# Attention layer on one core: swapping partitions by transfers, a later routing transpose, and one exponential for each quad of score banks

## The reference, cut to what matters

```
x  = L0_attn_x
xn = layernorm(layernorm(x)) * ln1_g + ln1_b
q  = rope(l2norm(xn @ Wq));  k = rope(l2norm(xn @ Wk));  v = xn @ Wv
clock = softplus(xn @ clock_w + clock_b)          # one per head
gcp = exp(clip(cumsum(-softplus(xn @ gate_w + gate_b)), -60, 50))
p_exp = exp(p - max(p)) * clock,  p = xn @ p_w + p_b
q = q * gcp / (cumsum(p_exp) + 1e-8)
k = k / (gcp + 1e-8) * p_exp
out = softmax(causal(q @ k.T / sqrt(8))) @ v @ out_w + out_b
x1 = out + residual;  y = x1 + mlp(layernorm(x1));  x = x + layernorm(y)
# the next layer routes each token to one of 8 experts: argmax(layernorm(x) @ centroids.T)
```

## Time and profile before

| what | value |
|---|---|
| median of 3 runs | 2163.32 us (2157.25 to 2165.94) |
| span of the profiled execution | 2164.4 us (no separate time is given for it beside its span) |
| attention's part of the span | from 0 to about 760 us |
| TensorE, VectorE, ScalarE, GpSimd busy, whole span | 85%, 79%, 68%, 54% |
| mean granted TensorE clock | 0.931 of full speed |

### The profile page before, as it was taken

One profiled execution on the slowest core, in us unless ns is written; L12 is line 12 of the kernel. 1 busy time (PEld: TensorE's weight loads), 2 busy tenths in 40 slices (PEclk: granted clock), 3 DMA queues, 4 the chain that ended last, 5 costly groups with the idle time before them and its releaser, 6 DMA issues. The chain is left out here.

```text
span 2164.4 us, 37241 instructions
## 1 busy us (share of the span) xinstructions
PE 1849.2 (85%) x12576; PEld 954.5 (44%) x12600; DVE 1703.8 (79%) x3547; ACT 1474.7 (68%) x2917; POOL 1165.1 (54%) x720
## 2 busy tenths in 40 slices
PE   6999999999998459957889889898898988659996
PEld 2566666656665259952222222222222222124453
DVE  7778868877863437854899999999999998976776
ACT  5888888888885138845656666666666666437775
POOL 2122232242221027871789999999999998840001
PEclk9999999999999669977899999999999998879998
DMA  4100010011001012221100111001111100023333
GB/s 169 36 26 26 28 49 26 26 36 41 21 25 33 20 50 77 88 72 42 30 25 27 34 35 34 27 30 30 31 35 35 35 31 30 21 67 90 97 84 78
DMA packets 103708, 97.35 MB, mean 45 GB/s; under 512 B 9137, under 2 KB 86113, under 8 KB 103137
## 3 DMA queue, kind: packets, MB, share of 16 engines
q1 hardware_dynamic: 95584, 75.34, 12.4%
q0 software_dynamic: 6784, 18.10, 2.5%
q10 hardware_dynamic: 1152, 1.54, 0.2%
HBM read 45.87 MB, written 28.10 MB: 34 GB/s over the span
## 5 line engine op out<-in xcount | busy, mean ns | idle before, releaser
L1935 POOL TENSOR_TENSOR hc<-h,c_rep 128x1024 f32<-128x1024 f32 x256 | 627.8, 2463 | 137.9 <-DVE h L1899 136.7
L1899 DVE TENSOR_TENSOR_SCAN h<-decay,bank 128x1024 f32<-128x1024 f32 x241 | 551.0, 2286 | 22.5 <-issue 0.9
L1757 ACT ACTIVATE decay<-bank,neg_a_r 128x510 f32<-128x510 f32 x512 | 322.6, 683 | 257.5 <-PE bank L1634 257.1
L1618 PE MATMUL bank<-u_in,sel_rows 32*128 32x512 f32 x964 | 287.9, 675 | 95.7 <-DVE h L1899 95.6
L1634 PE MATMUL bank<-delta,sel_rows 32*128 32x512 f32 x1024 | 338.8, 677 | 0.9 <-ACT decay L1757 0.9
L1886 DVE TENSOR_TENSOR bank<-bank,b_rep 128x1024 f32<-128x1024 f32 x241 | 291.2, 1208 | 34.8 <-PE bank L1618 33.0
L992 POOL DMA_INDIRECT rows_in_dram<-row,idx x64 | 63.3, 989 | 318.3 <-DVE row L965 303.7
L574 ACT ACTIVATE es<-bank 128x384 f32<-128x384 f32 x512 | 208.9, 499 | 22.1 <-PE bank L373 21.8
L1618 PEld LDWEIGHTS bank<-u_in,sel_rows 32*128 32x128 f32 x964 | 76.0, 191 | 276.7 <-DVE h L1899 199.7
L1649 PE MATMUL bank<-hc,y_sel 128*32 128x512 f32 x1024 | 149.6, 660 | 0.8 <-POOL hc L1935 0.8
L1656 PE MATMUL bank<-xpad,w_conv 128*128 128x512 f32 x256 | 133.0, 634 | 3.2 <-ACT xc L1819 1.6
(11 more groups left out here) (341 smaller groups left out, 4170.0 us busy)
## 6 DMA issues: line engine op xcount, KB each, us to landing
r_tw<-r_o_t SPq DMA_DIRECT2D x96, 128.0 KB, 2.3
xvs<-xv SPq DMA_DIRECT2D x16, 512.0 KB, 2.9
u_wide<-u_rep_dram SPq DMA_DIRECT2D x30, 256.0 KB, 3.5
xs<-rows_in_dram SPq DMA_DIRECT2D x72, 68.0 KB, 1.8
front<-in_x_dram SPq DMA_DIRECT2D x16, 256.0 KB, 2.9
w<-in_w_dram SPq DMA_DIRECT2D x2, 2048.0 KB
xlb_dram<-front SPq DMA_DIRECT2D x16, 256.0 KB, 2.3
xlb_m<-xlb_dram SPq DMA_DIRECT2D x16, 256.0 KB
```

Of the source, the lines that this page charges most:

```text
L1618: last = pe.matmul(BD[n % 2][:, i * STEP:(i + 1) * STEP], sel[at:at + 32, r, :], u_in[p if n < NS else q][at:at + 32, hf, :], start=True, ...
L1757: act.activation(decay[n % 4][:, i, :, 1:], seq(DL[i])[:, :, 1:], ACT.Exp, scale=c["neg_a_r"][:, hf, g:g + 1]).then_inc(s["n_da"], 1)
L1899: dve.tensor_tensor_scan(flat(h[n % RING]), decay[n % 4].rearrange("p i b t -> p (i b t)"), flat(drive_0) if by_pool else BD[n % 2], 0.0, ...
L1935: pool.tensor_tensor(hc[n % RING][:, :, :], h[n % RING][:, :, :], c_rep[p if n < NS else q][:, :].unsqueeze(1).to_broadcast([P, 2, STEP]), ...
```

## The change

The swapped projections go. `FA` is now multiplied by cos and by sin at once (`f_ra`, `f_rb`), SyncE exchanges the partitions of `rot_b` pairwise into a new buffer `rot_s` with two transfers (every second partition each way), and `f_rq` and `f_rk` subtract `rot_s`. In TensorE's order the q norm (L481) moves between `weigh(6)` and `weigh(7)`, the projection of k in front of `back(3)`, the routing transpose of xl2 behind `quad(2)`, the affinities behind the k norm, the ranks behind `quad(4)`. VectorE's and ScalarE's orders follow, and the routing's small instructions now stand together. The four exponentials of a quad are one over the four banks, and the quad raises `s_score` once, after its fourth bank. GpSimd's L985 waits for `m_xl2` too. `w_a` is loaded in three pieces without the two swapped blocks, and two small buffers of the end lie in `log`.

The diff, without the declarations, the changed counts of `p_small` (64 to 96) and `s_score` (32 to 8 a pair), and the `es` indexing in `weigh`:

```diff
+        def swap(sp, sem):
+            for to in range(2):
+                sp.dma_start(rot_s[to:P:2, :], rot_b[1 - to:P:2, :]).then_inc(sem, 16)
...
             if front:
+                sp.wait_ge(s["f_rb"], one_on)
+                swap(sp, s["f_qsw"])
+                sp.wait_ge(s["f_kb"], one_on)
+                sp.wait_ge(s["f_rq"], one_on)
+                swap(sp, s["f_ksw"])
                 sp.wait_ge(s["f_xlb"], one_on)
... pe_step
                 quad(7, k - 2, p)
-            if front:
-                pe.wait_ge(s["f_pe"], k + 1)
-                project(FB, c["w_qs"], s["f_qs"])
             if late:
                 weigh(6, k - 2, p)
+            if front:
+                pe.wait_ge(s["f_sq"], k + 1)
+                pe.wait_ge(s["f_rb"], k + 1)
+                pe.matmul(FA[:, :], c["ones_blk"], square[:, :], start=True, stop=True).then_inc(s["f_ssq"], 1)
+            if late:
                 weigh(7, k - 2, p)
             if scores:
                 quad(0, k - 1, q)
+            if front:
+                pe.wait_ge(s["f_pe"], k + 1)
+                project(FB, c["w_k"], s["f_k"])
             if late:
                 back(3, k - 2)
-            if front:
-                pe.wait_ge(s["f_sq"], k + 1)
-                pe.wait_ge(s["f_ra"], k + 1)
-                pe.matmul(FA[:, :], c["ones_blk"], square[:, :], start=True, stop=True).then_inc(s["f_ssq"], 1)
-                pe.wait_ge(s["f_rb"], k + 1)
-                project(FB, c["w_k"], s["f_k"])
...
                 quad(1, k - 1, q)
-            if front:
-                pe.wait_ge(s["f_mq"], k + 1)
-                project(FA, c["w_ks"], s["f_ks"])
             if scores:
                 weigh(0, k - 1, q)
+            if scores:
+                weigh(1, k - 1, q)
+                quad(2, k - 1, q)
             if tail:
                 pe.wait_ge(s["m_xl2"], k - 2)
                 transposes(M, xl2, s["m_x2t"])
-            if scores:
-                weigh(1, k - 1, q)
-                quad(2, k - 1, q)
... act_step
-                for st in range(HS):
-                    act.wait_ge(s["s_score"], u * 32 + HS * n + st + 1)
-                    if st == 0:
-                        since(act, s["s_av"], u * 8 + n - 1)
-                    last = act.activation(es[(n % 2) * HS + st][:, :], RING[st][:, 0:3 * P], ACT.Exp, scale=DH ** -0.5)
-                last.then_inc(s["s_exp"], 1)
+                act.wait_ge(s["s_score"], u * 8 + n + 1)
+                since(act, s["s_av"], u * 8 + n - 1)
+                act.activation(es[n % 2][:, :, :], ring[:, :, 0:3 * P], ACT.Exp, scale=DH ** -0.5).then_inc(s["s_exp"], 1)
... dve_step
                 dve.tensor_tensor(seq(rot), seq(FA), cos, ALU.mult).then_inc(s["f_ra"], 1)
+                since(dve, s["f_ksw"], 32 * k)
+                dve.tensor_tensor(seq(rot_b), seq(FA), sin, ALU.mult).then_inc(s["f_rb"], 1)
             if tail:
                 dve.wait_ge(s["m_st2"], k - 2)
                 bn_aggr(mv_m, stats_m, s["m_mv2"])
...
                 dve.scalar_tensor_tensor(pre[:, 0, :], pre[:, 0, :], 0.0, log[:, 0, :], ALU.max, ALU.add).then_inc(s["f_sp"], 1)
+                dve.wait_ge(s["f_ra"], k + 1)
+                dve.wait_ge(s["f_qsw"], 32 * k + 32)
+                dve.tensor_tensor(rot[:, :], rot[:, :], rot_s[:, :], ALU.subtract).then_inc(s["f_rq"], 1)
... pool_step
                 pool.wait_ge(s["f_back"], k + 1)
+                if tail:
+                    pool.wait_ge(s["m_xl2"], k - 2)
                 pool.tensor_tensor(mag[:, 1, :], mag[:, 1, :], one_up[:, :], ALU.subtract).then_inc(s["f_lost"], 1)
```

More of the change, by code:

```diff
@@ L232, in attention @@
         v_a = [sb(f"v_a{n}", [P, TS, H, 32]) for n in range(2)]
[L234 removed]
+        es = [sb(f"es{n}", [P, HS, 3 * P]) for n in range(2)]
         avs = sb("avs", [P, 512])
@@ L275, in attention @@
         end = sb("end", [1, E])
-        of = sb("of", [1, ETILES])
-        before = sb("before", [1, ETILES])
+        of, before = (log[0:1, 0, n * ETILES:(n + 1) * ETILES] for n in range(2))
         hi = sb("p_hi", [E * FC, P], bf16)
@@ L500, in pe_step @@
                 transposes(M, xl2, s["m_x2t"])
-            if scores:
-                weigh(1, k - 1, q)
-                quad(2, k - 1, q)
-            if tail:
-                pe.wait_ge(s["m_x2t_sb"], k - 2)
-                for j in range(TS):
-                    last = pe.matmul(M[:, j * E:(j + 1) * E], o_t[:, j * P:(j + 1) * P], c["cent"][:, :], start=True, stop=True)
-                last.then_inc(s["m_aff"], 1)
             if scores:
@@ L516, in pe_step @@
             if front:
-                pe.wait_ge(s["f_ka"], k + 1)
+                pe.wait_ge(s["f_kb"], k + 1)
                 pe.wait_ge(s["f_sk"], k + 1)
                 pe.matmul(FB[:, :], c["ones_blk"], square[:, :], start=True, stop=True).then_inc(s["f_ssk"], 1)
+            if tail:
+                pe.wait_ge(s["m_x2t_sb"], k - 2)
+                for j in range(TS):
+                    last = pe.matmul(M[:, j * E:(j + 1) * E], o_t[:, j * P:(j + 1) * P], c["cent"][:, :], start=True, stop=True)
+                last.then_inc(s["m_aff"], 1)
             if scores:
@@ L528, in pe_step @@
                 transposes(M, o_tok[p], s["m_ot"])
+            if scores:
+                weigh(2, k - 1, q)
+                quad(4, k - 1, q)
             if tail:
@@ L541, in pe_step @@
                 last.then_inc(s["r_rank"], 1)
-            if scores:
-                weigh(2, k - 1, q)
-                quad(4, k - 1, q)
             if mid:
@@ L815, in dve_step @@
                 bn_aggr(mv_m, stats_m, s["m_mv2"])
-            if front:
-                dve.wait_ge(s["f_qs"], k + 1)
-                since(dve, s["f_rk"], k)
-                dve.tensor_tensor(seq(rot_b), seq(FB), sin, ALU.mult).then_inc(s["f_rb"], 1)
             if tail:
@@ L906, in dve_step @@
                 dve.tensor_tensor(factor[:, :], factor[:, :], pcs[:, :], ALU.subtract).then_inc(s["f_zq2"], 1)
+            if front:
+                dve.wait_ge(s["f_ssk"], k + 1)
+                dve.wait_ge(s["f_zq"], k + 1)
+                dve.tensor_scalar(lnorm[:, :], FB[:, :], 1e-24, None, ALU.max).then_inc(s["f_mk"], 1)
+                dve.wait_ge(s["f_ka"], k + 1)
+                dve.wait_ge(s["f_ksw"], 32 * k + 32)
+                dve.tensor_tensor(rot_k[:, :], rot_k[:, :], rot_s[:, :], ALU.subtract).then_inc(s["f_rk"], 1)
+                dve.wait_ge(s["f_fq"], k + 1)
+                dve.wait_ge(s["f_rq"], k + 1)
+                since(dve, s["s_score"], 8 * k - 8)
+                dve.tensor_tensor(q_t[p][:, :], rot[:, :], factor[:, :], ALU.mult).then_inc(s["f_qt"], 1)
             if tail:
```

89 lines of the change are left out of this document (39 added, 50 removed).

## The result

The changed kernel takes 2193.91 us (median of 4 runs, 2190.81 to 2198.8) against 2162.13 us for the kernel before, measured beside it (4 runs, 2157.25 to 2165.94): a ratio of 1.0153, 95% interval 1.0133 to 1.0172, or +32 us. The forecast was +14. The sign was right and the time lay inside the range, but the predicted time missed by 17 us, more than the forecast change itself. It also lay above the 2190 that the forecast's own case reached; the range went higher only for the sake of rival D, which is not what happened in the steady steps. That it held is partly luck.

The account below looks back on a forecast made before the run. VectorE's unbroken queue was taken as the bound: -2.15 + 1.1 + 1.4 + 0.45 + 0.2 = +1.0 us a step, +13 over 13 steps, with -1 and +2 at the ends +14, 2177 us. Range 2140 to 2202 us.

Parts of the forecast that it names:

- the forecast's own case: VectorE's queue gets longer: 2177 us, own range 2168 to 2190, chance 0.47.
- rival D: Much slower: TensorE's pauses in a step let its clock fall, 2201 us, chance 0.08.
- Steps 0 to 2: First steps, without routing: no GpSimd collision lost before or after, projections save a little, -1 us together.
- the +2 for steps 16 to 18: Last steps: TensorE waits for the single exponential and the routing stands later, +2 us together.
- Items 1 and 2: VectorE's queue: xl2 freed from GpSimd's pair, -2.15 us a step; the late pair delays the second softplus sum, +1.1.
- Item 3: TensorE's q norm before `weigh(7)` and k projection before `back(3)`: `heads_rec(3)` waits for `back(3)`, +1.4 us a step.
- Item 4: VectorE's seven small routing instructions in a row take 1.25 us instead of 0.8 spread out: +0.45 us a step.
- Item 5: ScalarE's fused exponential: starts after the fourth mask matmul, quad 5's result later, +0.2 us at the step's end.
- Items 6 and 7: Removed k projection on TensorE gains nothing; the swap's transfers land in time: 0 us each on VectorE's queue.
- B: Faster: TensorE's new order costs VectorE nothing, step down 1.6 us, 2142 us in all; chance 0.23.
- C: No change that can be told: GpSimd does not hold up the running sum, 2163 us; chance 0.22.

Follow-up runs that it names:

- b3: Kernel before with the partition exchange by transfers in place of the two swapped projections, `w_a` loaded in three pieces, orders as before: ratio 1.0093.
- b4: b3 with GpSimd's pair waiting for xl2 too: ratio 0.9965 to the kernel before.
- d1: b3 with two projections of the removed size put back in their places, results unread: ratio 1.0024 to the kernel before.
- d2: b4 without the transfers, `rot_b` itself read for `rot_s`, so q and k differ from the reference: start 97.7 us.
- b1: Kernel before with only GpSimd's wait for xl2 added: ratio 0.9919, 2191.11 us beside 2210.36.
- c2: b4 with one exponential for each quad and the k projection ahead of `back(3)`, tail in the order of before: first steady step 41.72 us.
- a1: Changed kernel with the q norm put back behind `back(3)`: ratio 1.0087 to the kernel before, first steady step 42.48 us.
- a2: Changed kernel with the q norm put back behind `back(3)` in steps 0 to 2 only: one run of 2234.5 us, steady step 43.29.
- c1: a1 with VectorE's `rot_b` product put back behind the aggregation of x2's statistics: first steady step 42.48 us.
- a4: Changed kernel without GpSimd's wait for `m_xl2`: one run 2262.35 us beside 2209.14, ratio 1.024; first steady step 44.44 us.
- c4: b1 with VectorE's first product of the q factor moved ahead of the waiting softplus sum: that product takes 1.16 us for 0.68.

## Why the prediction was right in sign and wrong in size

**The step that failed** is the estimate "Steps 0 to 2 lack the routing, so lose L985's collision neither before nor after, and save a little of the projections: I estimate -1". It came out at +11.5 us in the first profile and +9.0 in the second (start 103.4 against 94.4). Like the +2 for steps 16 to 18 it had no row behind it, and it treated three filling steps as short steady ones. Everything that "lies beside other work" in a steady step was costed at nothing there too, and in steps 0 to 2 that cover is missing. The runs show three parts.

- The exchange with its waits: 4 to 6 us, in the steps 0 and 1 (b3, b4, d1), of which 4.0 stay without any transfer (d2 against b1).
- The k projection ahead of `back(3)` with the exponential: 1.9 us in step 2 (c2 against b4). The routing has no part in these steps.
- The rest, 2 to 4 us, is mostly the clock. From step 1 on every kernel without the exchange is granted 1.00; most of those with it get 0.90 to 0.96 over one or two of these steps, and such a step is 1.3 us longer for the same order: step 2 took 42.4 us at 1.00 in a1 and 43.7 at 0.96 in a2, 42.8 at 1.00 and 44.2 at 0.96 in the two profiles of the changed kernel. In step 0 of one order TensorE's last six projections took 3.19 us in a1 and 4.54 in c1, behind a pause of 3.1 us, and the step 28.2 and 29.6. So the changed kernel's early q norm with the waits behind it (4.41 us for ScalarE's square) looks dearer than it is: at equal clock it adds 0.4 us in step 2 and nothing in step 1 (32.1 us at 0.95, as in c2). Whether it makes the low clock likelier is open.

**The steady step** was right in mechanism and short by 0.45 us a step, 5.9 us over 13 steps. Its terms, in the order of the forecast:

- Items 1 and 2 together: -1.05 forecast, -1.0 measured alone (b1), and 1.15 when taken away again (a4). The start of L870 3.74 us behind the sum was forecast at 3.75. The rule of the Trainium skill (SBUF — State Buffer, Who interferes with whom) agrees with these traces: operations with two SBUF inputs and GpSimd block each other, those with at most one do not, outside VectorE's two-port modes (1.16 us in c4 and 0.66 in b1 beside the pair). It counts `tensor_scalar` among the instructions that can enter such a mode; here the clip and the four centrings of xl2, both of that kind, are held up beside the pair (0.86 us for 0.41, 3.27 for 1.11).
- Item 3: +1.4 forecast; 0.8 for the norm's place (a1) and up to 0.7 for the k projection's (c2, where the exponential has a part too) together make 1.5. Right.
- Item 4: +0.45 forecast, +0.76 measured (c1 less c2). The row itself was right, 1.22 us against 1.25 forecast, with 0.7 before and not 0.8. What was missing is the wait for the ranks behind quad 4 (0.24).
- Item 5: +0.2 forecast; 0 to 0.35 measured, depending on the order around it. ScalarE's busy time fell by 1.38 us a step, between the item's two estimates of 0.9 and 2.2, and gained nothing.
- Items 6 and 7: 0 forecast, +0.14 measured in the steady step (b4 less b1). The transfer is not waited for there. "If that cover were gone, each us late would be one on VectorE's queue" is what happened in step 1 of b4 (1.88 us); in the changed kernel the wait for the norm took its place.
- In all, each kernel's first steady step less the one named before it: -1.03 (b1), +0.14 (b4), +0.71 (c2), +0.76 (c1), +0.81 (after) is +1.39, from 41.90 to 43.29.
- Steps 16 to 18: +2 forecast, +0.6 measured (42.57 and 47.97 us against 42.33 and 47.63).

So of the 31.2 us lost up to the x2 of step 18 in the first profile, 19.2 are the steady part (1.45 x 13, and one step of 43.56), 11.5 the start and 0.6 the end. Against the forecast of +14 the start is 12.5 us too low, the steady part 5.9, and the end 1.4 too high.

**The rivals.** B and C fell: `back(3)` was late, and the running sum and GpSimd did hold each other up (GpSimd's first instruction 2.05 us for 1.27), so that L870 began only when the pair was done (444.93). D, the clock, stayed away in steady steps of the changed kernel (granted 1.00). But it was no idle fear: it appears in b3, 1.4 us a step, and in the start of the changed kernel (0.77 between 42 and 54 us).

## What to carry to other kernels

Cost the filling steps of a software pipeline by their own rows: what is hidden in the steady step is bare there, and three such steps were worth over a third of this result. Before bundling edits, run the one that has a row behind it alone; here one added wait was worth -0.8% and its companions turned it into +1.5%. Here the bound was one engine's unbroken queue: taking work from another engine gained nothing, and each new place in that engine's order had a price (0.8 us a step for one norm).

## What the runs showed of the hardware

- Taking 1.8 us of matmuls from a step made the step slower: the granted clock fell to 0.55 over 3.8 us, mostly TensorE's lower level of 1.2 GHz, behind a stretch with 9.64 us busy of 12.19 and a pause of 1.93, in seven of ten steps. With the work put back (11.14 busy, pause 1.04) it did not fall, nor without the work and with the pause gone (b4).
- A transfer of 128 KB between partitions took 2.1 us from issue to landing in the median and 3.8 us once, in step 1 of b4.
- In sixteen profiles from three chips ScalarE pauses 1.1 to 1.3 us at the start of most passes of its loop, in the two first profiles not; the cause is open.
